# The first layer's delta-rule scan: decay as a fifth row of the first product, and decay gates read later

## The reference, cut to what matters

```
def step(S, inp):
    qt, kt, vt, at, bt = inp
    Sk = jnp.einsum('bhde,bhe->bhd', S, kt)
    S_new = at * S - at * bt * outer(Sk, kt) + bt * outer(vt, kt)
    ot = jnp.einsum('bhd,bhde->bhe', qt, S_new)
    return (S_new, ot)
_, O = jax.lax.scan(step, S0, (q, k, v, a, bgate))
```

## Time and profile before

| | us |
|---|---|
| median of 3 runs | 1360.09 |
| the runs | 1351.15, 1360.18, 1360.09 |
| the profiled execution's own time | 1352.62 |
| its span, first to last instruction | 1350.9 |
| DVE busy in the span | 846.5 |
| PE busy | 989.0 |

### The profile page before, as it was taken

The page is one execution under the profiler, slowest core; times in us unless marked ns, Lnnn a source line. Parts: engine busy times, 40 slices in busy tenths (PEclk is TensorE's granted clock), DMA queues, the critical chain, the costliest instruction groups (busy, mean ns, idle before and its releaser), DMA issues.

```text
span 1350.9 us, 18007 instructions
## 1 busy us (share of the span) xinstructions
PE 989.0 (73%) x5924; PEld 600.3 (44%) x5924; DVE 846.5 (63%) x2008; ACT 623.9 (46%) x1485; POOL 442.6 (33%) x636
## 2 busy tenths in 40 slices
PE   5563074985886896888788888878788878775682
PEld 3231032443453454333334555544556545544582
DVE  1386978858988332675666566766566666624452
ACT  3435253464444253154444456643556534663272
POOL 0201352634633323022442331363241444422413
PEclk9776595996997998787888899987999988998796
DMA  7000000000000001000000323212134003331372
GB/s 221 1 0 1 0 0 1 1 1 35 1 1 1 1 0 36 1 1 1 1 1 1 114 71 105 75 36 92 33 111 122 29 18 120 106 107 46 125 218 80
DMA packets 53885, 64.67 MB, mean 48 GB/s; under 512 B 6544, under 2 KB 38304, under 8 KB 53792
## 3 DMA queue, kind: packets, MB, share of 16 engines
q1 hardware_dynamic: 51744, 59.33, 14.6%
q0 software_dynamic: 2048, 4.20, 1.0%
HBM read 52.83 MB, written 10.68 MB: 47 GB/s over the span
## 4 chain that ended last, share of the span: by engine, by line
PE 46%; DVE 19%; issue 13%; ACT 11%; POOL 8%; DMA 2%; SPq 0%; DVEq 0%; POOLq 0%; ACTq 0%
PE banks L701 8%; PE banks L844 4%; PE banks L758 4%; DVE MX L1323 3%; PE banks L554 3%; PE banks L776 3%; POOL oms L1796 3%; PE banks L748 2%; PE banks L818 2%; PE banks L711 2%; PE banks L714 2%; PE banks L606 2%; POOL QX L1695 2%; PE banks L723 2%; ACT PT L1620 1%
## 5 line engine op out<-in xcount | busy, mean ns | idle before, releaser
L1323 DVE TENSOR_REDUCE MX<-banks 128x4 f32<-128x512 f32 (+2 forms) x192 | 199.3, 1044 | 87.2 <-PE banks L818 86.5
L1774 POOL TENSOR_SCALAR_AFFINE_SELECT PT<-PT 128x256 f32<-128x256 f32 x256 | 107.0, 432 | 419.4 <-ACT PT L1620 419.1
L1620 ACT ACTIVATE PT<-banks 128x768 f32<-128x768 f32 (+1 forms) x192 | 167.9, 876 | 92.6 <-PE banks L776 91.5
L701 PE MATMUL banks<-xgT,wg 128*128 128x128 f32 x736 | 106.3, 290 | 36.1 <-ACT ysb L1581 29.5
L701 PEld LDWEIGHTS banks<-xgT,wg 128*128 128x128 f32 x736 | 92.5, 198 | 57.7 <-issue 53.0
L844 PE MATMUL banks<-PT,VA 128*17 128x512 f32 (+3 forms) x1024 | 98.4, 482 | 13.6 <-DVE on L1346 13.6
L783 PE MATMUL banks<-KS,QS 32*128 32x512 f32 (+3 forms) x512 | 96.7, 421 | 14.7 <-DVE MX L1323 12.3
L776 PE MATMUL banks<-QS,KS 32*128 32x128 f32 (+3 forms) x512 | 91.7, 407 | 15.0 <-ACT PT L1620 9.6
L748 PE MATMUL banks<-w,hid 128*128 128x128 f32 x512 | 76.1, 296 | 30.6 <-DVE hid L1268 28.5
L748 PEld LDWEIGHTS banks<-w,hid 128*128 128x128 f32 x512 | 69.6, 206 | 63.3 <-DVE hid L1268 43.9
L1272 DVE SCALAR_TENSOR_TENSOR sil<-sil,yh 128x256 f32<-128x256 f32 x124 | 53.4, 431 | 62.7 <-ACT sil L1567 62.4
(11 more groups left out here) (256 smaller groups left out, 2120.8 us busy)
## 6 DMA issues: line engine op xcount, KB each, us to landing
wg<-in_ffn_dram SPq DMA_DIRECT2D x92, 386.0 KB, 3.4
xg<-xs SPq DMA_DIRECT2D x20, 256.0 KB, 3.1
yb<-ysb SPq DMA_DIRECT2D x20, 256.0 KB, 3.9
w<-in_ffn_w_dram SPq DMA_DIRECT2D x12, 256.0 KB, 5.0
xs<-zt SPq DMA_DIRECT2D x1, 1472.0 KB, 11.1
x<-in_L_attn_x_dram SPq DMA_DIRECT2D x4, 256.0 KB, 5.0
out_dram<-x SPq DMA_DIRECT2D x16, 64.0 KB, 1.5
wmod<-in_L_wmod_dram SPq DMA_DIRECT2D x2, 384.0 KB, 4.1
```

The lines of the kernel that those rows point to most:

```text
L701: mm = e.matmul(ps[:, at:at + cols], w, h, start=True, stop=True)
L1323: v_mx.at(e.tensor_reduce(MX[n % 2][:, u:u + nm, qb % 2, 2 * pair:2 * pair + 2, 24].rearrange("p s i -> p i s"), p4, AX.X, ALU.max, negate ...
L1620: a_p.at(e.activation(PT[q % 3][:, 2 * pair:2 * pair + 2, :], where["score", q, pair][:, :, 0:n], ACT.Exp, scale=ISQ8))
L1774: ins = e.affine_select(out=pt, in_=pt, compare_op=ALU.is_ge, fill=0.0, base=0, pattern=[[0, 2], [1, 128]], channel_multiplier=-1)
```

## The change

The decay of a step is copied into `XU` once per block by ACT, as 8 equal numbers behind the keys and values of the 4 tokens (`gm_` of ACT, one instruction of 256 elements, signal `a_gx`). DVE's first product then has 5 rows: the fifth is state times decay. One buffer `TS` per step (three of them) holds everything: `T0` is the output of the first product (4 x 5 x 8), `T1` the 4 x 9 view that the first reduction reads, `T2` the second product's output, now with the tokens before the 8 columns (4 x 4 x 8), and `T3` the view of decay row and second product together that the second reduction reads: 5 terms, 8 numbers (32 bytes) apart. The second product therefore reads `KT` with its 8 columns innermost, 4 numbers (16 bytes) apart. ACT writes only the values, now 2 steps ahead instead of 3, and waits for `v_w` instead of `v_s`. The wait of DVE for `a_ts` is gone.

`LATE0` for DVE changes: `ab` 1 to 6, `route` 1 to 2, `o_x` 1 to 2. In DVE's order this puts `ab` of the fourth block behind steps 18 and 19 of the first (it stood before step 18), and `o_x` part 0 behind step 16. In ACT's order `gm_` comes between step 19 and the scaling into `hTr`. `otok` and `xt` now lie in the memory of `OL`, with a wait for `v_x1` in each `o_ol`.

```diff
-    DVE=dict(mod=1.0, gate=1.0, ab=1.0, up=5.0, route=1.0, o_x=1.0),
+    DVE=dict(mod=1.0, gate=1.0, ab=6.0, up=5.0, route=2.0, o_x=2.0),
...
-        T1 = [sb(f"T1{i}", [128, 4, 4, 9], where=st) for i in range(4)]
-        T2 = [sb(f"T2{i}", [128, 4, 8, 5], where=st) for i in range(2)]
+        TS = [sb(f"TS{i}", [128, 4, 76], where=st) for i in range(3)]
+        T0 = [t[:, :, 0:45].rearrange("p r (j e) -> p r j e", e=9)[:, :, :, 0:8] for t in TS]
+        T1 = [t[:, :, 0:36].rearrange("p r (j e) -> p r j e", e=9) for t in TS]
+        T2 = [t[:, :, 44:76].rearrange("p r (j e) -> p r j e", e=8) for t in TS]
+        T3 = [t[:, :, 36:76].rearrange("p r (j e) -> p r e j", e=8) for t in TS]
...
+                U5 = XUf[g % 2][:, 56 * c:56 * c + 60].rearrange("p (j x) -> p j x", x=12)[:, :, 0:8]
...
+                    v.wait_ge(a_gx, g + 1)
...
-                n = v_own.at(e.tensor_tensor(T1[k1][:, :, :, 0:8], S_[:, c, :, :].unsqueeze(2).broadcast_to([128, 4, 4, 8]),
-                                             XU[:, c, :, 0:8].unsqueeze(1).broadcast_to([128, 4, 4, 8]), ALU.mult))
+                n = v_own.at(e.tensor_tensor(T0[k1], S_[:, c, :, :].unsqueeze(2).broadcast_to([128, 4, 5, 8]),
+                                             U5.unsqueeze(1).broadcast_to([128, 4, 5, 8]), ALU.mult))
...
-                n = v_own.at(e.tensor_tensor(t2[:, :, :, 0:4], W_[:, c, :, :].unsqueeze(2).broadcast_to([128, 4, 8, 4]),
-                                             KT[:, c, :, :].unsqueeze(1).broadcast_to([128, 4, 8, 4]), ALU.mult))
+                n = v_own.at(e.tensor_tensor(T2[k1], W_[:, c, :, :].unsqueeze(3).broadcast_to([128, 4, 4, 8]),
+                                             KT[:, c, :, :].rearrange("p e j -> p j e").unsqueeze(1)
+                                             .broadcast_to([128, 4, 4, 8]), ALU.mult))
                 v.wait_ge(v_own, n)
-                v.wait_ge(a_ts, j + 1)
...
-                v_s.at(e.tensor_reduce(Sn, t2[:, :, :, :], AX.X, ALU.add))
+                v_s.at(e.tensor_reduce(Sn, T3[k1], AX.X, ALU.add))
...
+            def gm_(g):
+                a.wait_ge(v_gm, g + 1)
+                a.wait_ge(v_s, 32 * (g - 1))
+                a_gx.at(e.activation(XUc[g % 2][:, :, 48:56], GMb[g % 2][:, :, 3:4].broadcast_to([128, 32, 8]), ACT.Copy))
...
             def scan(g, c):
                 j = 32 * g + c
                 if c == 0:
-                    for k in range(3):
-                        values(j + k)
-                a.wait_ge(v_gm, g + 1)
-                a.wait_ge(g_zero, 1)
-                a.wait_ge(v_s, j)
-                a_ts.at(e.activation(T2[c % 2][:, :, :, 4], Sb[g % 2][:, c, :, :], ACT.Copy, scale=GMb[g % 2][:, c, 3:4]))
-                if c + 3 < 32:
-                    values(j + 3)
+                    values(j)
+                    values(j + 1)
+                if c + 2 < 32:
+                    values(j + 2)
```

More of the change, by code:

```diff
@@ L334, in build @@
         GMb = [sb(f"GM{i}", [128, 32, 4], where=st) for i in range(2)]
-        XUb = [sb(f"XU{i}", [128, 32, 4, 12], where=st) for i in range(2)]
+        XUf = [sb(f"XU{i}", [128, 32 * 56 + 4], where=st) for i in range(2)]
+        XUc = [t[:, 0:32 * 56].rearrange("p (c x) -> p c x", x=56) for t in XUf]
+        XUb = [t[:, :, 0:48].rearrange("p c (j x) -> p c j x", x=12) for t in XUc]
         KTb = [sb(f"KT{i}", [128, 32, 8, 4], where=st) for i in range(2)]
-        T1 = [sb(f"T1{i}", [128, 4, 4, 9], where=st) for i in range(4)]
-        T2 = [sb(f"T2{i}", [128, 4, 8, 5], where=st) for i in range(2)]
+        TS = [sb(f"TS{i}", [128, 4, 76], where=st) for i in range(3)]
[3 more added lines that the diff above has]
+        T3 = [t[:, :, 36:76].rearrange("p r (j e) -> p r e j", e=8) for t in TS]
         Wb = [sb(f"Wb{i}", [128, 32, 4, 4], where=st) for i in range(2)]
@@ L344, in build @@
         PR = sb("PR", [128, 32, 3, 12], where=st)
-        otok = sb("otok", [128, 4, 8, 16], where=st)
+        otok = OL[:, :, :, :].rearrange("p c j e -> p (c j e)")[:, 0:512].rearrange("p (b x h) -> p b x h", x=8, h=16)
         oT = sb("oT", [128, 512], where=st)
@@ L349, in build @@
         tok = [sb(f"tok{w}", [128, (4, 8, 4)[w], 2, 64], where=st) for w in range(3)]
-        xt = otok[:, :, :, :].rearrange("p b x h -> p b (x h)")
+        xt = OL[:, :, :, :].rearrange("p c j e -> p (c j e)")[:, 0:512].rearrange("p (b d) -> p b d", b=4)
         st.close()
@@ L424, in build @@
             signal(n) for n in ("v_dk", "v_gm", "v_vb", "g_pr", "v_ga", "v_xu", "g_kt"))
-        g_zero, a_val, a_ts, v_w, v_s = (signal(n) for n in ("g_zero", "a_val", "a_ts", "v_w", "v_s"))
+        g_zero, a_val, a_gx, v_w, v_s = (signal(n) for n in ("g_zero", "a_val", "a_gx", "v_w", "v_s"))
         g_gq, g_qx, g_ol, v_ol, p_o, p_ol, a_os, p_tok, a_ot, p_ot, a_oT, p_wo, v_xt, v_x1 = (
@@ L631, in o_turn @@
                 for b in range(4):
-                    tr = e.transpose(ps[:, 128 * b:128 * b + 128], otok[:, b, :, :].rearrange("p x h -> p (x h)"), ident[:, :])
+                    tr = e.transpose(ps[:, 128 * b:128 * b + 128], xt[:, b, :], ident[:, :])
                 p_ot.at(tr)
@@ L1132, in gm_ @@
                 v.wait_ge(v_dk, g + 1)
-                v.wait_ge(a_ts, 32 * (g - 1))
+                v.wait_ge(a_gx, g - 1)
                 v.wait_ge(g_gq, g - 1)
@@ L1186, in scan @@
                 j = 32 * g + c
-                k1, t2, XU, KT = j % 4, T2[c % 2], XUb[g % 2], KTb[g % 2]
+                k1, KT = j % 3, KTb[g % 2]
+                U5 = XUf[g % 2][:, 56 * c:56 * c + 60].rearrange("p (j x) -> p j x", x=12)[:, :, 0:8]
                 S_, W_ = Sb[g % 2], Wb[g % 2]
@@ L1241, in o_ol @@
                 v.wait_ge(p_ol, g)
+                v.wait_ge(v_x1, g)
                 v_ol.at(e.tensor_tensor(
@@ L1505, in values @@
                 a.wait_ge(v_xu, g + 1)
-                a.wait_ge(v_w, j - 3)
-                a_val.at(e.activation(T1[j % 4][:, :, :, 8].rearrange("p r j -> p j r"), XUb[g % 2][:, c, :, 8:12],
+                a.wait_ge(v_w, j - 2)
+                a_val.at(e.activation(T1[j % 3][:, :, :, 8].rearrange("p r j -> p j r"), XUb[g % 2][:, c, :, 8:12],
                                       ACT.Copy, scale=-1.0))
@@ L1530, in o_tok @@
                 a.wait_ge(v_x1, g)
-                a_ot.at(e.activation(otok[:, :, :, :].rearrange("p b x h -> p x b h"),
+                a_ot.at(e.activation(otok.rearrange("p b x h -> p x b h"),
                                      bank[7][:, :].rearrange("p (x b h) -> p x b h", x=8, b=4), ACT.Copy))
@@ L1633, in _ @@
             jobs = dict(mod=mod, lam=lam_, tok=tok_, diag=diag, norm=norm, route=route, qkv=qkv, decay=decay, conv=conv,
-                        turned=turned, k_t=k_t, vq_t=vq_t, ab_t=ab_t, scan=scan, o_sum=o_sum, o_tok=o_tok, o_turn=o_turn,
+                        turned=turned, k_t=k_t, vq_t=vq_t, ab_t=ab_t, gm=gm_, scan=scan, o_sum=o_sum, o_tok=o_tok, o_turn=o_turn,
                         gate_t=gate_t, up=up, turn=turn, keep=keep, down=down, qk_in=qk_in, v_in=v_in, score=score, o_back=o_back, rms_t=rms_t)
@@ L1726, in o_ol @@
                 g_.wait_ge(p_ol, g)
+                g_.wait_ge(v_x1, g)
                 g_ol.at(e.tensor_tensor(
```

2 lines of the change are left out of this document (1 added, 1 removed).

## The result

The changed kernel is slower. Its median is 1363.18 us (20 runs, 1360.26 to 1373.79) against 1352.07 us for the kernel before on the same chip (20 runs, 1347.95 to 1361.18): a ratio of 1.0076, with a 95% interval from 1.0058 to 1.0093. That is +10.3 us where −7 was forecast. The profiled execution took 1361.46 us, its span is 1359.6.

A forecast was written before the change was run, and what follows sets the result against it. DVE was taken as nearest to full, held where ACT stands behind other queued work. Gains 17.75 less 1.6 for `hTr` give 16.1 us; cost 9.2; net −6.9, taken as −7: 1353 us from the 1360.1 median, range 1337 to 1369.

The forecast's parts named there:

- The gain: Scan, block by block: DVE reaches fixed jobs earlier, 3.25, 5.7, 6.2 and 2.6 us in blocks 1 to 4, 17.75 together.
- the `hTr` term: ACT's `gm_` delays the scaling into `hTr` queued behind it: +1.0 us in block 2, +0.6 in block 3.
- Block 1: DVE held by `dk`, which needs ACT's `AB`: `dk` starts 3.5 us earlier, 3.25 us gained after paying for `ab`.
- Block 2: `AB` there at 202.95 against a `dk` at 208.76: 5.7 us gained, with 0.1 for the hand-over.
- The price of a step: Three changed DVE instructions: first product +0.03 us, second product +0.09, second reduction +0.01, together +0.13 us a step.
- rival (a): Second reduction slowed at L1220's rate, 85 steps times 0.11 us more: net +2.4 us, 1362.5; chance 0.20.
- The steps on the path: Steps on the chain: 22 in block 1, 16 each in blocks 2 and 3, 14 in block 4; 68 at 0.13, 8.8 us.
- The cover that the forecast named: Steps off the chain cost nothing, except 17 before L1250 in block 4, which come out 0.4 us late against their cover.
- PE's full stretch in block 3: From 249 to 288 us PE is the chain in 96% of the time, so DVE's waits for ACT there bring nothing.
- L998 waits for the router: In the changed profile, DVE waits about 1 us for PE's router product.
- Values two steps ahead: ACT's values, 2 steps ahead instead of 3 and tied to `v_w`, cost nothing while ACT is less than two steps late.
- Rival (d): The wait is only renamed: DVE waits for values in ACT's queue, leaving only the prices, about +9 us, 1369; chance 0.08.

The follow-up runs named there:

- The kernel that has the whole gain side and none of the price: Kernel before without ACT's decayed state (decay left out) and with the three new DVE latenesses: 1345.40 us, ratio 0.9882; on another chip 1337.84 us, ratio 0.9889.
- The price alone: Kernel before, ACT's decay and old latenesses kept, only T2 stored as 4 x 5 x 8, so second product and second reduction read strided: 1379.33 us, ratio 1.0144.
- DVE's own decay: Kernel before, old layouts, DVE instead of ACT making the decayed state by one extra instruction per step, new latenesses: 1350.75 us, ratio 0.9988; again 0.9946; 36-number forms 0.9967, 0.9964.

## Why the prediction was wrong

**What bounds the kernel: right.** Half or more of DVE's waits on ACT bring nothing, and the gain had to be read in differences at fixed jobs.

**The gain, 17.75 us before the `hTr` term: within the error by the medians, too large in the scan.** The kernel that has the whole gain side and none of the price is 15.0 us faster on one chip and 16.1 us (0.0118 of 1361.94) on the other, and both intervals hold 17.75. Its scan is 9.4 and 11.3 us shorter, little more than half; where the medians' other 4 to 7 us come from is not shown. Block 1 was forecast well: `dk` 3.5 us earlier. In the three traces with a free chain, the new latenesses, no strided read and a clock above 0.50 it comes 3.5 or 3.6 us earlier (51.0, 51.1 and 51.1 for 54.6), in the three others, at 0.50, by 1.9 to 2.8 us. Block 2 was forecast too high. With it `dk` should have come 9.2 us earlier in all; in the two traces of the kernel without decay it came 5.2 and 3.9 us earlier (129.3 and 130.6 us after the scan's start, for 134.5).

**The price of a step: the term that failed.** Forecast +0.03, +0.09 and +0.01, together 0.13 us. Measured, as totals over 128 steps: +0.031, +0.091 and +0.118, together 0.240. The first two, priced from instructions of the same kind and pattern in the earlier trace rows, are right to 1 ns. The third was priced from a one-input copy of 32 numbers, and stood at the lower end of a range whose upper end, 0.12, was the truth. The reason given, that the pattern of L1135 is the nearest, was poor: it is another instruction, with 32 numbers beside a fixed time of some 180 ns. At the 0.73 ns a number of the reduction those 32 would have added 23 ns, and the row has 8; why the copy pays less is not shown. L1220, which the forecast used only as the upper bound, had the rate. This is the price of rival (a), which had a chance of 0.20. That its 1362.5 us lie beside the measured 1363.18 is luck: it forecast +2.4 us on a median of 1360.1, and +10.3 were measured on 1352.07. For the same reason 1363.18 stands inside the range 1337 to 1369, which as differences reads −23 to +9 us. The Trainium skill, "SBUF — State Buffer", section "Door 1: The DMA port swizzle", which was cited beside it, notes that each access to another 16-byte line pays. Both strided instructions agree (383 ns for 292, 437 for 320).

**The steps on the path: the second failure.** The forecast put 68 of 128 steps on the chain, and cover on the rest. Counted from each scan's start, the changed kernel takes 25.2 to 27.2 us more than the one without decay, of 30.8 us of added DVE time (82 to 88%); by the medians it is 28 (91%). The price alone, on the kernel before, arrives with 19.6 of about 27 us (73%), or 21.0 in the scan. So it is as if some 95 to 115 steps lay on the chain. The cover that the forecast named did not hold for work that is added in every step. Under PE's full stretch in block 3 the step's four instructions had no share of the chain before and have 36% of it now, and with both reads in order that share is gone again. L1260 was to start when PE's L648 ends: it does in block 2, but in block 3 L648 ends at 305.58 us and L1260 starts at 307.74, and in block 4 it is 404.05 and 404.77.

**The two failures in the sum.** The forecast's cost was 9.2 for the steps and 1.6 for `gm_` and `hTr`, 10.8 in all; 28 were measured. Of the 17.2 us missing, the reduction's 0.107 us by 95 to 115 steps is 10 to 12, and the 0.13 us by 27 to 47 steps that were counted as covered is 4 to 6. Gain 15, price 28 give +13; the two direct measurements of the change, 1.0076 and 1.0095, are +10.3 and +12.9.

**The smaller points.** `AB` bound DVE in block 1 and L648 in block 2, as said, but L648 did not in block 3. L998 waits for the router 1.3 us (forecast about 1). Values two steps ahead were not free: 4.2 us in 4 waits. Rival (d), the renamed wait, is thereby small; its cost alone would have been these 4.2.

**The intermediate theory.** The kernel without decay and with the old order first gave 0.9978, and I took the gain for 3 us. The same kernel gave 0.9946 on another chip, and the latenesses added another 8 us to it there, 3.5 of them in the scan. Its scan was 6.1 us shorter in the first trace already. A part was taken for the whole, and one ratio with an interval of half a per cent for its middle.

## What to carry to other kernels

- When a change swaps the loop order of a buffer, price each instruction that reads it at its new stride, from a row with the same number of inputs and at least as many elements. A copy of 32 numbers showed 8 ns here where the rate of the larger instructions makes 23. If there is no such row, take the far end of the range for the forecast too when the instruction stands in every step.
- Of the time added to every step of this chain, which runs on the busiest engine, 73 to 91% arrived, though a fifth of the stretch looked like waiting. Waits removed gave 9 to 16 of 45 us. The two don't trade one for one.
- Count a stage from its own start. The scan started 72.5 to 77.1 us into the span, so end times alone mislead by up to 5 us, and a single span by what the 918 to 934 us behind the scan happened to take.
- An instruction on which the next one does not depend costs next to nothing between two dependent ones (0.25 us for 0.03), but look at what else it contends with. The versions with DVE's own decay are the fastest here that keep the decay, at ratios of 0.9946 to 0.9988, and clearly faster than the changed kernel. Against the kernel before they gain at most half a per cent, and two of the four intervals reach 1.

## What the hardware showed

- A reduction of 160 numbers takes 437 ns reading 32 bytes apart, 320 in order: 0.73 ns a number more. A two-input product of 128 numbers with one input 16 bytes apart takes 383 for 292: 0.71 ns a number. The two rates are nearly the same, one input or two, 16 bytes or 32.
- DVE's two-input products and its one-input product with a per-partition factor take up to 1.2 to 2.0 us for 0.25 to 0.38 where POOL is at work; its reductions never do (454 ns at most in L1218, 322 in the one in order). The Trainium skill, "SBUF — State Buffer", section "Who interferes with whom", says that a product with two SBUF inputs waits for a GpSimd instruction that reads SBUF and that reductions on this chip never do. The traces agree. It also says that a one-input product can take both of DVE's ports when its operands meet further conditions, and contends then too. In the two forms tried here, 32 numbers and 9 rows against one row of 36, it waited (maxima 2040 and 2043 ns); whether by such a mode is not shown.
- TensorE's granted clock took a part of block 1's gain in the changed kernel. From 110 to 125 us it was at 0.50, the lower of its two levels, through the whole stretch, where it was 0.71 in the kernel before; PE was busy 7.6 of those 15 us, before 7.0. In all 17 traces the way in block 1 from PE's last but one product for `wqkv` (L535 in the kernel before) to ACT's `AB` takes one of two times: 5.3 us or, in the nine traces at 0.50, 7.7. That is 2.4 us of the 3.8 by which `AB` comes later in the changed kernel, counted from the scan's start (54.8 for 51.0 us). The strided reads are not needed for it: all six traces with a strided read are at 0.50, but so are three of the eleven without. The kernel in which DVE decays the state has 0.50 in one trace and 0.66 in the other. There `dk` is only 0.9 us apart, since the slower way starts 1.5 us earlier. What brings the clock to 0.50 in that stretch is open.
